# Two self attention stages of a long single-core kernel: the loop over head parts put outside the loop over row groups in two matmul blocks, and one wait in place of several

## The reference, cut to what matters

```python
def _L1_xattn_ref(x, context, w_q, b_q, w_k, b_k, w_v, b_v, w_o, b_o):
    N_HEADS = 16
    DIMS = 256
    HEAD = DIMS // N_HEADS
    q = x @ w_q + b_q
    k = context @ w_k + b_k
    v = context @ w_v + b_v
    ...
    scale = 1.0 / np.sqrt(HEAD).astype(np.float32)
    scores = jnp.einsum('bqhd,bkhd->bhqk', q, k) * scale
    weights = jax.nn.softmax(scores, axis=-1)
    out = jnp.einsum('bhqk,bkhd->bqhd', weights, v).reshape(B, Lq, D)
    return out @ w_o + b_o
...
x = x + _L0_xattn_ref(_layernorm(x, axis=-1), ctx_768, ...)   # 8 heads of 64, no biases on q, k, v
x = x + _L0_ffn_ref(...)
x = x + _L1_xattn_ref(_layernorm(x, axis=-1), ctx_768, ...)   # 16 heads of 16
...
```

## Time and profile before

| | |
|---|---|
| time, median of 3 runs | 5437.33 us (5433.27 to 5439.6) |
| the profiled execution | 5442.26 us |
| its span (first to last instruction) | 5440.5 us |
| TensorE busy over the span | 84% |
| VectorE busy over the span | 67% |
| ScalarE, GpSimd busy | 41%, 9% |
| scores L471 | 1536 matmuls, starting between 45.3 and 1073.5 us |
| products with the values L487 | 1536 matmuls, starting between 59.4 and 1093.6 us |

### The profile page before, as it was taken

How to read it: one execution, slowest core, us unless ns; L and a number is a source line. 1 busy time by engine, 2 the same in 40 slices (tenths; PEclk the granted TensorE clock), 3 DMA queues, 4 the chain that set the end, 5 groups by cost and what they waited for, 6 DMA issues and landing times. The chain is left out here.

```text
span 5440.5 us, 73347 instructions
## 1 busy us (share of the span) xinstructions
PE 4549.9 (84%) x23536; PEld 3433.6 (63%) x23536; DVE 3632.9 (67%) x8277; ACT 2216.0 (41%) x5225; POOL 499.1 (9%) x926
## 2 busy tenths in 40 slices
PE   6991699989996999999999999999922687878786
PEld 5770577756663777777777777778701455555554
DVE  4556666655555777777777777777664778777545
ACT  2330233334443556555555555555531222222332
POOL 0003100011003000000000000000030121212210
PEclk9995799989997999999999999999955788888789
DMA  1001000000000000000000000000002000000100
GB/s 56 0 0 21 31 0 0 0 1 0 0 0 15 2 2 4 2 3 2 4 2 4 2 4 2 4 2 2 4 10 57 1 0 0 0 0 0 34 0 31
DMA packets 43602, 41.33 MB, mean 8 GB/s; under 512 B 15610, under 2 KB 39806, under 8 KB 43266
## 3 DMA queue, kind: packets, MB, share of 16 engines
q1 hardware_dynamic: 43332, 38.08, 2.5%
HBM read 33.61 MB, written 4.19 MB: 7 GB/s over the span
## 5 line engine op out<-in xcount | busy, mean ns | idle before, releaser
L1203 DVE TENSOR_TENSOR global_prob_t_low<-psum,global_prob_t_high 128x512 fp32r<-128x512 f32 x960 | 657.1, 690 | 252.1 <-ACT global_prob_t_high L1295 238.0
L1295 ACT ACTIVATE global_prob_t_high<-psum 128x512 fp32r<-128x512 f32 x960 | 569.7, 600 | 613.7 <-PE psum L1409 613.7
L1209 DVE TENSOR_REDUCE global_top<-psum 128x1 f32<-128x480 f32 x1024 | 667.1, 658 | 135.1 <-PE psum L1369 129.8
L1316 ACT ACTIVATE global_prob<-psum,global_bias 128x480 f32<-128x480 f32 x1024 | 674.1, 662 | 17.9 <-DVE global_bias L1212 15.1
L1409 PE MATMUL psum<-ident,global_prob 128*128 128x128 f32 x3840 | 568.8, 273 | 36.5 <-DVE global_prob_t_low L1203 35.4
L1409 PEld LDWEIGHTS psum<-ident,global_prob 128*128 128x128 f32 x3840 | 468.4, 141 | 196.1 <-DVE global_prob_t_low L1203 68.1
L1367 PE MATMUL psum<-global_prob_t_high,global_v_low 128*128 128x512 f32 x960 | 455.8, 475 | 0.8
L1367 PE MATMUL psum<-global_k_high,global_q_low 128*128 128x480 f32 x1024 | 393.8, 385 | 19.4 <-ACT global_prob L1316 11.9
L1368 PE MATMUL psum<-global_k_low,global_q_high 128*128 128x480 f32 x1024 | 392.5, 383 | 12.4 <-issue 12.4
L1369 PE MATMUL psum<-global_k_high,global_q_high 128*128 128x480 f32 x1024 | 395.3, 386 | 0.0
L188 POOL TENSOR_TENSOR rstd<-mean_var,eps 128x1 f32<-128x1 f32 x225 | 49.5, 220 | 3646.2 <-DVE mean_var L182 3631.4
(11 more groups left out here) (399 smaller groups left out, 8769.2 us busy)
## 6 DMA issues: line engine op xcount, KB each, us to landing
x_res<-in_x SPq DMA_DIRECT2D x4, 1024.0 KB, 9.7
moe_we<-in_expert_t SPq DMA_DIRECT2D x8, 512.0 KB, 7.7
out<-x_res SPq DMA_DIRECT2D x4, 1024.0 KB, 8.4
cho_wqkv<-in_L_ffn_Wqkv SPq DMA_DIRECT2D x2, 1536.0 KB
self_ctx_t<-in_ctx_t SPq DMA_DIRECT2D x2, 1440.0 KB
sel_w<-in_L_xattn_W SPq DMA_DIRECT2D x2, 1024.0 KB, 12.7
global_ctx_t<-in_ctx_t SPq DMA_DIRECT2D x1, 1440.0 KB
sel_ctx_t<-in_ctx_t SPq DMA_DIRECT2D x1, 1440.0 KB
```

The costliest lines, as they stand in the source:

```text
L1203: dve.tensor_tensor(dst, psum, high.bitcast(F32), ALU.subtract).then_inc(ready.sem, 1)
L1209: ins = dve.tensor_reduce(top[:, c:c + 1], w.psum[:, c, 0:chunk], AX.X, ALU.max)
L1295: act.activation(dst, psum, ACT.Copy).then_inc(ready.sem, 1)
L1316: act.activation(prob[:, par, j, c * chunk:(c + 1) * chunk], w.psum[:, c, 0:chunk], ACT.Exp, bias=bias[:, j % 2:j % 2 + 1], scale=scale, a ...
```

## The change

In the block of the scores and in that of the products with the values, the loop over the parts k is put outside and the loop over the row groups r inside. The wait for the copies of the transposed probabilities, before one for each row group, becomes one ahead of both loops, for the last row group's copy. Signals, operands, banks and partitions stay as they are.

```diff
-                        for r in range(per):
-                            for k in range(parts):
+                        for k in range(parts):
+                            for r in range(per):
                                 rows = slice(r * pad, (r + 1) * pad)
                                 last = pe.matmul(w.psum[:, r, k * NCTX:(k + 1) * NCTX],
                                                  q_t[rows, k, :], k_t[rows, k, :], start=True, stop=True)
...
-                        for r in range(per):
-                            pe.wait_ge(prob_t_ready.sem, prob_t_ready.count(t * per + r))
-                            for k in range(parts):
+                        pe.wait_ge(prob_t_ready.sem, prob_t_ready.count(t * per + per - 1))
+                        for k in range(parts):
+                            for r in range(per):
                                 h = k * per + r
                                 last = pe.matmul(w.psum[r * pad:(r + 1) * pad, 4, k * P:(k + 1) * P],
                                                  v[:, h * pad:(h + 1) * pad], prob_t[:, r, k, :],
```

## The result

The changed kernel takes 5468.81 us, the median of 8 runs (5448.48 to 5480.64), beside 5437.93 for the kernel before (8 runs, 5433.27 to 5441.77). The ratio is 1.0057, 95% interval 1.0041 to 1.0073: slower by about 31 us, where 16 us faster was forecast. The profiled execution took 5480.64 us, the slowest of the eight, with a span of 5478.8. The runs of the changed kernel also spread over 32 us, those of before over 8.5.

The account below looks back on a forecast made before the run. TensorE's order was taken to bound short V turns, a chain ending in GpSimd's copy short K turns, VectorE most of long turns. Short stage 15.5 plus long 3.5 - 2.5 = 1 saves 16.5 us: 5437.33 to 5421, range 5410 to 5442.

Parts of the forecast that it names:

- The scores: Score matmuls: row groups start 0.05 us apart instead of 0.55; short stage 1.20 instead of 1.70, saving 0.50 per turn.
- The products with the values and the one wait: Products with the values, short stage: waiting for the last copy loses 0.03 us per V turn, nothing in K turns.
- The long stage, no gain in the middle: Long stage: V turns gain nothing, K turns 0.05 to 0.1 us; with first and last turns 3.5 us together.
- The clock: Long stage: wider gap before the transposes halves TensorE's clock in 3 V turns at 0.9 us, 2.5 us lost.
- the clock: Rival: long stage drops to half clock in V and K turns, 40 us lost against 19 gained, 5458; chance 0.12.
- Overlap doesn't grow: Rival: in the scores row groups overlap no more than before, 5434 to 5439 us, no visible change; chance 0.17.
- switching costs: Rival: in scores and products with the values every row group change shows its fill, 200 us lost, 5637; chance 0.06.
- the long stage gains: Rival: TensorE, not VectorE, sets the long stage, so another 32 x 1.5 us is saved, 5373; chance 0.05.
- The prediction's sentence on strict program order: Scores: quoted skill rule that matmuls start strictly in program order; by it alone today's 16 would last 1.95 us.

Follow-up runs that it names:

- e3: Kernel before with the new loop order in the scores alone, both stages; 5429.31 us, ratio 0.9985.
- e11: Kernel before with the new loop order in the scores of the short stage alone; 5420.52 us, ratio 0.9968.
- e14: Kernel before with only the one wait for the last copy, loop orders old; 5510.30 us, ratio 1.0118.
- e5: Changed kernel plus unread 512-column products ahead of the transposes (long stage) and ahead of L501 (K turns, both stages); 5383.64 us, ratio 0.9903.
- e1: Kernel before with the whole change (both loop orders and the one wait) in the short stage alone; 5424.53 us, ratio 0.9979.
- e10: Kernel before plus unread products 8 columns wide in both gaps; 5427.71 us, ratio 0.9980.
- e12: Kernel before with new score loops in both stages, values as before, plus the wide unread products in both gaps; 5390.31 us, ratio 0.9910.
- e13: Changed kernel with the products with the values back in the old loop order behind the one wait; 5473.15 us, ratio 1.0092.

## Why the prediction was wrong, by its own steps

**The scores: right.** 1.20 and about 1.25 were forecast with a stagger of 0.05 between row groups; 1.16 and 1.17 were measured, which leaves 0.02 for all of it. Eight matmuls of a group at 0.112, a first that shows 0.37, and nothing more: 0.10 + 7 x 0.112 + 0.27 = 1.15. The Trainium skill, page "TensorE: Matmul & The Clock Gate", Part 3, has tiles of different row groups start about 4 ns apart; the trace nearly agrees, with three more groups in 0.02, which is 7 ns for each. The saving is 0.54 per short turn, for 0.50 forecast, and e3 and e11 show it without disturbance: 17.3 and 16.2 us.

**The products with the values and the one wait: right in the V turn, if the order is there.** No loss (10.04 in e3, with the old values, and 10.05 with both), for 0.03 forecast; their wait is 0.74 and they last 1.09. L203 stands 0.54 earlier in the turn than in the earlier trace rows. e14 prices the wait without the order: 0.49.

**The long stage, no gain in the middle: right.** With the clock held its turns are 14.79 and 15.85 (e5) against 14.83 and 15.91 in the earlier trace rows. In its first turn 2.5 us were won (13.70 in place of 16.18), where 1.5 was forecast.

**"The clock": this step failed.** It said that the gap is at the edge and that the change makes it 1.5 us wider, priced a drop in a V turn at 1.0 and then counted three. The price was right: L203 goes 9.08 after the start of the turn at 924.77, 9.14 had been worked out, and the turn is 15.79. The count was wrong: all 15 V turns of the long stage have the drop (11 at 15.5 to 15.8, four worse), which costs about 25 us in place of 2.5. And the sum had V turns alone. It put new or longer drops in the K turns at nothing, with no reason in this step; they cost 28 us in the long stage and 9.6 in the short one. The reason that I gave for a low count, that a later turn meets the drop at another place, holds for e3, where 9 of 15 V turns keep the clock, but not once the values are denser too. In e3 and in the changed kernel the wait is the same 2.65; what differs is how long the touched groups last in the turn. I had looked only at the gap that grows, and not at everything in the turn that shrinks. What a turn contains does not decide alone either. The three slow K turns of the short stage start at 182.27, 271.19 and 360.12, and those of e1, with the same short stage, at 120.70, 209.64 and 362.93, among turns that are alike to 0.01 us. So it also matters when a turn falls, and the exact condition stays open.

**The rival "the clock" is what came, and it was also mis-sized.** It gave 5458 and had a chance of 0.12. Its price for a K turn was at most 1.7, taken from a stretch of 3.42 at half clock. The stretches that begin ahead of L501 last 6.8 in both stages and cost 3.2 in the short one and 2.8 to 3.2 in the long one. Those of 10.24 begin within the transposes and cost 2.5 to 2.7 in K turns and 3.8 in the four worst V turns; one K turn, with 13.65 at half clock, costs 3.6. The argument against it, "the short stage, with smaller gaps, never drops", was read off a kernel whose touched groups were longer: its gap ahead of L501 is 1.00 in both the earlier trace rows, and three K turns drop all the same. That is 9.6 us of the short stage's 17.1. The Trainium skill, page "TensorE: Matmul & The Clock Gate", has in its section "Why this matters for your kernels" the rule that gaps between bursts send TensorE back to its slow clock, and it spoke for this rival. The traces agree with it in direction, but the length of the gap alone doesn't foretell the drop here (e3 beside the changed kernel in the long stage, before beside after in the short one).

**The other rivals.** Overlap doesn't grow, switching costs, the long stage gains: all refuted by the same rows (1.16, 1.17; 14.79 at full clock). "Where the code lies" was in no rival.

The span adds up so: short stage -7.5, long stage +49.9, experts +4.6, global attention -5.7, the rest -3.0, in all +38.3.

## What to carry to other kernels

Before making TensorE's small matmuls denser, ask whether TensorE or another engine sets the turn: where it is another, the time saved is idle time, and more than that can be paid back when the granted clock falls over the work behind it. Look at the clock by turns, in the kernel before and over all kinds of turn; here one kind at 0.89 and the other at 1.00 came before both went. Where a swap of loops is free in one stage and dear in another, make it in the one (e11), or fill the gaps with products that nobody reads (e5) and compare both kernels filled, since only that shows what the swap itself is worth.

## What the runs showed of the hardware that was not expected

**Row groups overlap fully if the program alternates between them.** In program order by groups, a second group starts about 0.55 after the first and 32 matmuls take 2.79; alternating, they take 1.17, at 37 ns for each, the groups 7 ns apart. Nor do the matmuls of different groups start in program order in the kernel before: in the scores at 203.36 the second group's first matmul, told by its longer record of 0.367, starts 0.548 after the first group's first, ahead of that group's last three at 0.654, 0.765 and 0.877. The prediction's sentence on strict program order is not borne out there.

**Denser use of the array can cost clock.** The long stage went from a mean of 0.93 at 441 us busy to 0.82 at 410, with the same matmuls. Density isn't the only way to it: with the old orders and the one wait (e14) it is 0.78.

**Code that isn't touched changes its time.** The global attention takes 2257.5 to 2268.5 us in the kernels without extra products and 2239 to 2245 in all seven with them, wide or narrow. In five of its rounds in the kernel before, some 276 us apart, TensorE stands still for 2.1 to 2.8 us within a group of score matmuls, and nothing in the profile releases it. Timeline of TensorE, the kernel before:

```profile
2309.71 0.47 PE L1367 MATMUL psum<-global_k_high,global_q_low 128*128 128x480 f32 x1 [1.69 <-ACT global_prob L1316]
2313.01 0.56 PE L1368 MATMUL psum<-global_k_low,global_q_high 128*128 128x480 f32 x1 [2.82 <-issue]
2313.36 0.60 PE L1369 MATMUL psum<-global_k_high,global_q_high 128*128 128x480 f32 x1
```

With each, a stretch of 6.8 us at half clock begins within 0.6 us of the start of the stop, and which of the two brings the other is open. In the kernels with extra products these stops are missing. Since narrow products do it as well, the array's time isn't the cause; that it is where the added instructions push the later code is an inference, and no run tests it by itself. It matters for reading e5 to e10 and e12: some 18 to 29 us of their gain are this, and only the stages' own windows tell it from the effect of the clock. The experts' stage, also untouched, takes 559 to 574 us, by how long it begins at half clock (the first 16 to 50 us of it). The extra products don't decide that: it takes 567.9 with them in e12 and 561.4 without them in e13. Why it differs is open.
